# The attention's loop of four turns over three groups of heads, written out as twelve groups of straight code

## The chip, the cores and the metric

The kernel runs on one core of a Trainium2 chip. The metric is the device time of one execution in microseconds. Before the change three runs gave a median of 1996.15 us (1995.97 to 1996.78). The execution that the profiler recorded took 1994.75 us, of which 1992.6 us are the span from the first to the last instruction.

## The reference

Two blocks work on `x` of shape (4, 1024, 512) in float32. The first is a conditioned feed-forward block. The second is attention with 16 heads of width 32 over 1024 positions, with no mask:

```python
qkv = (h @ Wqkv.T + bqkv).reshape(B, N, num_heads, hd, 3)
energy = jnp.einsum('bhqd,bhkd->bhqk', q, k)
att = jax.nn.softmax(energy, axis=-1) / D ** 0.5
out = jnp.einsum('bhqk,bhkd->bhqd', att, v)
out = out @ Wp.T + bp
h1 = out + hidden
h2 = _sln(h1, w, ln_g, ln_b, Wg, bg, Wb, bb)
return h2 + h1
```

## The kernel before

The kernel has five stages one behind the other: setup, the feed-forward block (L0), the projection to q, k and v, attention, and the output projection with its normalization. Each stage gives every engine a program of its own; engines meet only at semaphores. No scheduler orders anything: the order on an engine is the order of the code.

Attention treats 64 (batch, head) pairs in 16 groups of four heads. One group is 16 steps, eight blocks of 128 keys for each of two halves of 512 queries. In a step PE (TensorE) does, in `group` of `attention_stage`:

- four energy products (`energies`, L1220), each into one PSUM bank, which ACT (ScalarE) turns into `probs` with an exponential (L1349);
- four products for the row maxima (`max_unit`, L1204), reduced by DVE (VectorE) at L1371, which run 13 steps ahead of the energies that use them, so that the last 13 steps of a group work on the maxima of the next one;
- the product with v of the step before (`av`, L1232), and half of a sum of the denominators (`den`, L1248), whose input POOL (GpSimd) adds up pairwise at L1468.

SP (SyncE) issues the transfers: the next q, k and v, and the detour of the maxima and denominators through other layouts. Three sets of buffers (`RING = 3`) are used in turn, so group g works in slot (g + 2) mod 3.

All five engines walk through the 16 groups with one helper, `groups(eng, group)` at L1080 to L1092. Group 0 stands alone. Groups 1 to 12 are a hardware loop of four turns (`eng.Fori(0, 4)`, L1087), whose body holds three groups, one for each slot. Groups 13 to 15 stand alone behind it. In the loop the group number is a register, so each wait for a value that depends on it needs register instructions ahead of it, at the line of the wait (L1203, L1219 and so on for PE). At the end of a turn an engine adds one to its counter and jumps back with a compare-and-branch, both recorded at L1087. The engines turn back each for itself, when its own code reaches the end; nothing joins them there.

Of the kernel before, what the change touches and what calls it, by code (L numbers as in the profile page):

```python
# [1000 lines left out]
def attention_stage(nc, sh, wp_t):  # L1001
# [11 lines left out]
    with ExitStack() as ctx:  # L1013
# [68 lines left out]
        def groups(eng, group):  # L1082

            group(0, 2, nth=0, first=True)
            with eng.Fori(0, 4) as k:  # L1087
                for i in range(RING):
                    group(3 * k + i + 1, i, nth=k + (i + 2) // RING)
            group(13, 0, nth=4)  # L1090
            group(14, 1, nth=5, load=False)
            group(15, 2, load=False, with_next=False)  # L1092
# [14 lines left out]
        def _(sp):  # L1107
# [76 lines left out]
            place_neg(0, RING - 1, 0)  # L1184
            load_group(2, 1)
            groups(sp, group)
            for half in range(QH):
                store(G - 1, half)
# [7 lines left out]
        def _(pe):  # L1196
# [111 lines left out]
            pe.wait_ge(ones_col_ready, 1)  # L1308
            pe.wait_ge(stack_loaded[RING - 1], LOADS)
            groups(pe, group)  # L1310
            av(G - 1, RING - 1, STEPS - 1)
            den(G - 1, PAIRS - 2, range(PARTS))
# [12 lines left out]
        def _(act):  # L1325
# [35 lines left out]
            act.wait_ge(wp_loaded, 16)  # L1361
            nc.scalar.copy(sh.wp[:, HI], wp_raw[:]).then_inc(wp_split, 1)
            groups(act, group)
            take_av(G - 1, 1)
            take_den(G - 1, 1)
# [384 lines left out]
```

## Time and profile before

| | before |
|---|---|
| median of 3 runs | 1996.15 us |
| the profiled execution | 1994.75 us |
| its span | 1992.6 us |
| PE busy | 1902.4 us, 95% |
| DVE busy | 1209.5 us, 61% |
| POOL busy | 1147.9 us, 58% |
| ACT busy | 809.2 us, 41% |
| DMA, mean over the span | 107 GB/s |
| granted TensorE clock, mean | 0.972 |

Busy time is the union of an engine's instructions. PE is busy for nearly the whole span, so what counts is how much of its time it stands still, and how much of it runs at the lower of its two clock levels. The granted clock is a share of 2.4 GHz: 1.00 is 2.4 GHz, 0.50 is 1.2 GHz, and a value between them is a stretch with a part at each. PE here means the matrix products and PEld the loading of their stationary operand, which runs beside them. An engine name with a q, as SPq or PEldq, stands for its sequencer, whose register, branch and semaphore instructions are not counted as busy.

### The profile page before, as it was taken

The numbers are of one execution on the slowest core, as the hardware profiler recorded it, in microseconds if no ns is written. First come the engines' busy times: TensorE is split into PE (matmuls) and PEld (weight loads), VectorE is DVE, ScalarE is ACT, GpSimd is POOL, SyncE is SP. The second block draws the span as 40 slices with busy tenths as digits, with TensorE's granted clock in tenths as the row PEclk, the third lists the DMA queues.
The fourth block names the chain that finished last, engine by engine and source line by source line (L and its number), as shares of the span: only waits on it lengthen the run. The fifth ranks groups of instructions, "written<-read, shape, count | busy, mean of one in ns | idle before, by whom it ended". The sixth has DMA issues, their size and how long they took to land. (4 is left out here: it accounts for less than half of the span.)

```text
span 1992.6 us, 31072 instructions
## 1 busy us (share of the span) xinstructions
PE 1902.4 (95%) x10520; PEld 1243.4 (62%) x10520; DVE 1209.5 (61%) x1510; ACT 809.2 (41%) x1373; POOL 1147.9 (58%) x589
## 2 busy tenths in 40 slices
PE   6599999999998999998999999999999999999995
PEld 1478888888886888885445544554554545554584
DVE  3556555655646554446666666666666666664289
ACT  1322123112312222221566656666666666666300
POOL 0574465466445121212477777777777777877545
PEclk9799999999999999997899999999999999999997
DMA  6301110101123555566344422344443334405293
GB/s 240 123 1 53 45 41 21 53 32 39 35 74 101 190 188 181 189 198 175 73 97 108 103 67 77 96 102 98 107 103 78 78 83 102 107 24 181 92 392 123
DMA packets 117704, 212.67 MB, mean 107 GB/s; under 512 B 18599, under 2 KB 36135, under 8 KB 117577
## 3 DMA queue, kind: packets, MB, share of 16 engines
q1 hardware_dynamic: 98828, 200.04, 33.7%
q10 hardware_dynamic: 18560, 10.94, 1.9%
q8 instruction: 78, 1.28, 0.3%
q14 instruction: 46, 0.37, 0.1%
q0 software_dynamic: 192, 0.05, 0.0%
HBM read 134.40 MB, written 75.80 MB: 105 GB/s over the span
## 5 line engine op out<-in xcount | busy, mean ns | idle before, releaser
L1371 DVE TENSOR_REDUCE at_mrow<-banks 128x1 f32<-128x1024 f32 x512 | 604.4, 1217 | 281.2 <-PE banks L1204 281.2
L1349 ACT ACTIVATE at_probs<-banks 128x512 f32<-128x512 f32 x1024 | 557.6, 597 | 333.7 <-PE banks L1220 314.4
L1468 POOL TENSOR_TENSOR at_pair<-at_probs 128x2048 f32<-128x2048 f32 x127 | 582.0, 4583 | 176.8 <-ACT at_probs L1349 176.7
L1220 PE MATMUL banks<-early_qs,early_ks 98*128 98x512 f32 x1024 | 443.8, 436 | 5.5 <-ACT at_probs L1349 5.5
L1204 PE MATMUL banks<-early_ks,early_qs 96*128 96x512 f32 x1024 | 377.5, 413 | 13.3 <-DVE at_mrow L1371 9.7
L1220 PEld LDWEIGHTS banks<-early_qs,early_ks 98*128 98x128 f32 x1024 | 192.4, 189 | 211.6 <-ACT at_probs L1349 106.8
L1232 PE MATMUL banks<-at_probs,at_v 128*32 128x512 f32 x2048 | 274.9, 609 | 0.9 <-ACT at_probs L1349 0.9
L1204 PEld LDWEIGHTS banks<-early_ks,early_qs 96*128 96x128 f32 x1024 | 199.1, 197 | 53.4 <-DVE at_mrow L1371 26.7
L67 PE MATMUL banks<-l_ht,l_weights 128*128 128x512 f32 x768 | 178.8, 392 | 5.5 <-ACT l_gt L574 5.5
L67 PE MATMUL banks<-qk_nt,l_weights 128*128 128x512 f32 x768 | 177.1, 392 | 3.0 <-ACT qk_gt L889 3.0
L67 PE MATMUL banks<-l_weights,l_hf 128*128 128x512 f32 x768 | 177.3, 390 | 0.0
L574 ACT ACTIVATE l_gt<-banks,mod 128x512 f32<-128x512 f32 x64 | 48.1, 778 | 314.3 <-PE banks L468 278.7
L67 PEld LDWEIGHTS banks<-l_ht,l_weights 128*128 128x128 f32 x768 | 144.6, 189 | 35.6 <-issue 5.8
L67 PEld LDWEIGHTS banks<-qk_nt,l_weights 128*128 128x128 f32 x768 | 145.3, 189 | 33.5 <-ACT qk_gt L889 3.2
L67 PEld LDWEIGHTS banks<-l_weights,l_hf 128*128 128x128 f32 x768 | 143.7, 188 | 29.5
L1248 PEld LDWEIGHTS banks<-at_pair,at_ones_col 128*32 128x32 f32 x2032 | 66.3, 110 | 138.9 <-issue 133.0
L1248 PE MATMUL banks<-at_pair,at_ones_col 128*32 128x256 f32 x2032 | 151.1, 381 | 0.0
L988 POOL TENSOR_TENSOR qk_nt<-qk_gt,qk_nt 128x512 fp32r<-128x512 f32 x32 | 43.0, 1363 | 156.2 <-DVE qk_nt L940 156.2
L898 ACT ACTIVATE qk_out<-banks,cols 128x512 fp32r<-128x512 f32 x64 | 44.1, 690 | 192.5 <-PE banks L67 186.4
L700 POOL TENSOR_TENSOR l_ht<-l_gt,l_ht 128x512 fp32r<-128x512 f32 x64 | 84.3, 1318 | 62.7 <-DVE l_ht L616 62.7
L583 ACT ACTIVATE l_gt<-banks,cols 128x512 f32<-128x512 f32 x96 | 64.7, 689 | 105.0 <-POOL l_hf L700 51.0
L700 POOL TENSOR_TENSOR l_hf<-l_gt,l_hf 128x512 fp32r<-128x512 f32 x64 | 82.7, 1293 | 40.6 <-DVE l_hf L616 40.6
(120 smaller groups left out, 1955.3 us busy)
## 6 DMA issues: line engine op xcount, KB each, us to landing
qk_scratch<-qk_out SPq DMA_DIRECT2D x64, 512.0 KB, 2.8
early_ks<-qk_scratch SPq DMA_DIRECT2D x48, 512.0 KB, 6.7
early_qs<-qk_scratch SPq DMA_DIRECT2D x96, 256.0 KB, 11.6
attn_scratch<-at_out SPq DMA_DIRECT2D x32, 512.0 KB, 2.7
o_a<-attn_scratch SPq DMA_DIRECT2D x32, 512.0 KB, 11.0
v_scratch<-qk_v ACTq DMA_DIRECT2D x32, 256.0 KB, 2.4
at_v<-v_scratch SPq DMA_DIRECT2D x16, 512.0 KB, 14.6
o_x<-x_scratch SPq DMA_DIRECT2D x8, 1024.0 KB, 14.3
```

The lines of the kernel that those rows point to most:

```text
L67: last = pe.matmul(out, stationary(a), moving(b), start=start and n == 0, stop=stop and n == len(TERMS) - 1)
L574: nc.scalar.activation(gt[:, k % 2, :], half[k][:], ACT.Identity, bias=sh.mod[:, 2 * which + 1, k, bass.ds(b, 1)], scale=sh.mod[:, 2 * whi ...
L583: nc.scalar.activation(gt[:, n % 2, :], halves[n][:], func, bias=sh.cols[:, col + m:col + m + 1]).then_inc(gt_full, 1)
L700: nc.gpsimd.tensor_tensor(dst[:, LO, i, :], gt[:, i % 2, :], dst[:, HI, i, :].bitcast(F32), ALU.subtract).then_inc(gt_lo, 1)
L898: nc.scalar.activation(qk[:, m, HI, :], ps[m][:], ACT.Identity, bias=sh.cols[:, C_BQ + m:C_BQ + m + 1]).then_inc(qk_hi, 1)
L1204: pe.matmul(e_ps[u % 2][:, keys, :], qs[0:96, slot, half, j, c * P:(c + 1) * P], ks[0:96, slot, j, keys * CH:(keys + 1) * CH], start=True, ...
L1220: pe.matmul(et[j % 2][:], ks[0:98, slot, j, (i % KC) * P:(i % KC + 1) * P], qs[0:98, slot, i // KC, j, :], start=True, stop=True).then_inc ...
L1232: last = pe.matmul(av_ps[rows, :], v[:, slot, kc, rows], probs[:, kc % 4, j, :], start=kc == 0, stop=kc == KC - 1)
L1248: last = pe.matmul(den_ps[HD * j:HD * (j + 1), cols], ones_col[:], psum2[:, pair % 2, j, cols], start=n == 0 and part == 0, stop=n == KC / ...
L1349: nc.scalar.activation(probs[:, i % 4, j, :], et[j % 2][:], ACT.Exp).then_inc(exp_done, 1)
L1371: nc.vector.tensor_reduce(mrow[:, half, u:u + 1], e_ps[u % 2], AX.XY, ALU.max).then_inc(max_done, 1)
L1468: nc.gpsimd.tensor_tensor(psum2[:, pair % 2], probs[:, a], probs[:, a + 1], ALU.add).then_inc(pair_ready, 1)
```

## The change

One line of the helper changes, for all five engines alike. The four turns are no longer a loop of the hardware: Python's `range` runs when the program is built, and the twelve groups are emitted one behind the other, with group numbers that are constants.

```diff
@@ -1084,7 +1084,7 @@
             group(0, 2, nth=0, first=True)
-            with eng.Fori(0, 4) as k:
+            for k in range(4):
                 for i in range(RING):
                     group(3 * k + i + 1, i, nth=k + (i + 2) // RING)
             group(13, 0, nth=4)
```

The program of PE before, at the back edge of the loop (the last step of a turn, the counter, the branch, and the first products of group 13, which the last turn falls through to):

```order
L1219 REGISTER_ALU
L1220 MATMUL banks<-early_qs,early_ks 128x512
L1203 REGISTER_ALU
L1204 MATMUL banks<-early_ks,early_qs 128x512
L1219 REGISTER_ALU
L1220 MATMUL banks<-early_qs,early_ks 128x512
L1204 MATMUL banks<-early_ks,early_qs 128x512
L1087 REGISTER_ALU
L1087 COMPARE_AND_BRANCH
L1204 MATMUL banks<-early_ks,early_qs 128x512
L1220 MATMUL banks<-early_qs,early_ks 128x512
```

The program of PE now, at the place where the last step of a group meets the first of the next:

```order
L1220 MATMUL banks<-early_qs,early_ks 128x512
L1204 MATMUL banks<-early_ks,early_qs 128x512
L1220 MATMUL banks<-early_qs,early_ks 128x512
L1204 MATMUL banks<-early_ks,early_qs 128x512 x2
L1220 MATMUL banks<-early_qs,early_ks 128x512
L1204 MATMUL banks<-early_ks,early_qs 128x512
L1220 MATMUL banks<-early_qs,early_ks 128x512
```

The products and their order are the same; counter, branch and the register instructions are gone. On ACT the head of the loop before reads as follows (`at_probs` is the exponential of an energy bank, `at_av_sb` the copy of the product with v):

```order
L1349 ACTIVATE at_probs<-banks 128x512 x16
L1087 UNCONDITIONAL_BRANCH
L1087 ISA
L1346 ISA
L1348 ISA
L1349 ACTIVATE at_probs<-banks 128x512
L1348 REGISTER_ALU
L1349 ACTIVATE at_probs<-banks 128x512
L1328 ISA
L1331 REGISTER_ALU
L1332 ACTIVATE at_av_sb<-banks 128x512
L1348 REGISTER_ALU
```

ACT's program now at the same place:

```order
L1349 ACTIVATE at_probs<-banks 128x512 x18
L1332 ACTIVATE at_av_sb<-banks 128x512
L1349 ACTIVATE at_probs<-banks 128x512 x14
L1339 COPY at_den_sb<-banks 128x512
L1349 ACTIVATE at_probs<-banks 128x512 x18
```

Here too no activation moves; the register instructions between them are gone. The straight form of a group is not new to the program: groups 0 and 13 to 15 had it before.

## Rows read from the trace of the kernel before

**Rows 1.** The page: span, and busy time of each engine.
```profile
span 1992.6 us, 31072 instructions
PE 1902.4 (95%) x10520; PEld 1243.4 (62%) x10520; DVE 1209.5 (61%) x1510; ACT 809.2 (41%) x1373; POOL 1147.9 (58%) x589
```

**Rows 2.** Waits from 1009 to 1867 us: who waited for whom, total, times, longest.
```profile
ACT at_probs L1349 <- PE banks L1220: 273.6, 274, 2.6
DVE at_mrow L1371 <- PE banks L1204: 260.9, 231, 3.2
...
PE banks L1204 <- DVE at_mrow L1371: 6.6, 3, 2.3
PE banks L1220 <- ACT at_probs L1349: 5.5, 12, 0.6
```

**Rows 3.** Stretches, groups 1 to 14, each from its first energy product (columns named).
```profile
core 0: us, PE busy (x) PEld busy (x) DVE busy (x) ACT busy (x) POOL busy (x), PEclk, DMA share, GB/s
1009.45:1065.99 56.54, 56.54 (x387) 28.35 (x387) 38.86 (x39) 36.71 (x69) 43.66 (x14) 1.00 0.39 95
...
1122.53:1181.58 59.05, 56.79 (x387) 28.40 (x387) 40.14 (x39) 37.07 (x69) 46.55 (x16) 1.00 0.39 91
1181.58:1239.68 58.10, 58.10 (x388) 28.76 (x386) 37.77 (x38) 36.36 (x68) 41.27 (x13) 0.97 0.38 93
...
1296.22:1355.10 58.88, 56.78 (x388) 28.40 (x388) 40.04 (x39) 37.07 (x69) 46.46 (x16) 1.00 0.37 92
1355.10:1413.14 58.04, 58.04 (x388) 29.12 (x386) 37.76 (x38) 36.48 (x68) 41.29 (x13) 0.97 0.39 93
...
1469.68:1528.69 59.01, 56.79 (x388) 28.39 (x387) 40.04 (x39) 37.07 (x69) 46.39 (x16) 1.00 0.37 91
1528.69:1585.19 56.50, 56.50 (x387) 28.34 (x386) 37.76 (x38) 36.37 (x68) 41.34 (x13) 1.00 0.39 96
...
1698.27:1754.80 56.53, 56.53 (x388) 28.35 (x387) 38.84 (x39) 36.72 (x69) 43.79 (x14) 1.00 0.39 95
1754.80:1811.32 56.52, 56.52 (x387) 28.34 (x387) 38.83 (x39) 36.71 (x69) 44.09 (x14) 1.00 0.09 30
sum 801.87, PE 795.29 PEld 398.21 DVE 544.35 ACT 514.14 POOL 616.94; mean PE 56.81 PEld 28.44 DVE 38.88 ACT 36.72 POOL 44.07
```

**Rows 4.** Timeline of PE at the first branch: start, us, instruction, idle before, releaser.
```profile
1178.37 0.40 PE L1220 MATMUL banks<-early_qs,early_ks 98*128 98x512 f32 x1
1178.61 0.39 PE L1204 MATMUL banks<-early_ks,early_qs 96*128 96x512 f32 x1
1181.26 0.49 PE L1204 MATMUL banks<-early_ks,early_qs 96*128 96x512 f32 x1 [2.26 <-DVE at_mrow L1371]
```

**Rows 5.** Line L1087: durations in ns (least, median, most), first and last start.
```profile
L1087 PEldq COMPARE_BRANCH  x4: 83/3636/3732, 1177.2 to 1696.4; - x4
L1087 ACTq COMPARE_BRANCH  x4: 40/53/53, 1178.9 to 1698.1; - x4
L1087 DVEq COMPARE_BRANCH  x4: 50/56/63, 1179.1 to 1698.3; - x4
L1087 POOLq COMPARE_BRANCH  x4: 40/45/45, 1179.6 to 1698.8; - x4
```

**Rows 6.** Timeline of DVE at the first branch.
```profile
1179.03 1.23 DVE L1371 TENSOR_REDUCE at_mrow<-banks 128x1 f32<-128x1024 f32 x1 [1.17 <-PE banks L1204]
```

**Rows 7.** Stretches of one step: undisturbed, and the first behind each of three branches.
```profile
1239.68:1243.20 3.52, 3.52 (x25) 1.76 (x25) 2.34 (x3) 2.76 (x6) 2.87 (x2) 1.00 0.13 22
1181.58:1186.68 5.10, 5.10 (x25) 2.18 (x24) 1.26 (x2) 2.42 (x5) 4.20 (x2) 0.67 0.17 43
1355.10:1360.19 5.09, 5.09 (x26) 2.57 (x25) 1.26 (x2) 2.66 (x5) 4.22 (x2) 0.66 0.33 64
1528.69:1532.20 3.51, 3.51 (x26) 1.76 (x24) 1.27 (x2) 2.43 (x5) 3.51 (x2) 1.00 0.13 40
```

**Rows 8.** DMA queues that carry instructions: packets, MB, share of 16 engines.
```profile
q8 instruction: 78, 1.28, 0.3%
q14 instruction: 46, 0.37, 0.1%
```

## The prediction

> **What bounds the kernel now.** I read the page's busy times first. PE is busy for 1902.4 of 1992.6 us, no other engine for more than 1209.5 us [rows 1]. In the attention the waits confirm who leads: ACT stood 273.6 us and DVE 260.9 us waiting for PE, while PE stood 6.6 us behind DVE, in three pieces, and 5.5 us behind ACT, in twelve [rows 2]. So PE sets the pace, and only what makes PE idle or slows it can move the time.
>
> Then I laid one stretch over each group, from the first energy product of one group to that of the next [rows 3]. All hold the same work (387 or 388 products), so their lengths may be compared. Two are straight code already: group 13 takes 56.53 us and group 14 takes 56.52 us. In the loop group 1 takes 56.54 us, and of the twelve looped groups seven lie between 56.50 and 56.54. Five are longer: group 3 (59.05), 4 (58.10), 6 (58.88), 7 (58.04) and 9 (59.01). The loop turns back at the ends of groups 3, 6 and 9; at the end of group 12 it falls through. The long groups are exactly those that end or begin at a taken branch.
>
> The timeline of PE shows what happens there [rows 4]. The product that starts at 1178.61 is the last of its turn's code; the next starts at 1181.26, with 2.26 us of idle time ahead of it. The rows of the branch give the reason [rows 5]: on PE's sequencer the compare-and-branch has a median of 3636 ns and a most of 3732 ns over four, and the least is 83 ns. One of the four is not taken, three are. The first began at 1177.2 and so lasted until 1180.9; the sequencer had run ahead of the array, and the array worked off what was queued, until 1179.0, before it stood.
>
> **Whether the branch is the cause.** The trace names a DVE reduction (L1371) as the releaser of the 2.26 us. This must be decided, because if PE truly waited for DVE, the wait would stay when the branch goes. The code speaks against it: `max_unit` n waits for reduction n - 2 only, as two pairs of banks are in use. The reduction that stands next to the stall ran from 1179.03 to 1180.26 [rows 6] and belongs to the product that ended at 1179.0, thus, if the next unit is n, to unit n - 1. The one that was needed lay before it. Even the later one was over 1.0 us before PE restarted. The branch, over at 1180.9, fits the restart at 1181.26.
>
> **The change part by part.**
>
> 1. *Three taken branches on PE.* The groups that end at one are longer than group 13 by 59.05 - 56.53 = 2.52, 58.88 - 56.53 = 2.35 and 59.01 - 56.53 = 2.48 us. Sum 7.35 us. Of this, the idle time is 6.6 us, the three pieces [rows 2]; the rest is the slower restart of the first products (0.49 us instead of 0.39 for the first [rows 4]). All of it is on the path, since PE is what the others wait for.
>
> 2. *The clock behind the branches.* Right behind the stall of the first and second branch the granted clock falls: the first step of group 4 takes 5.10 us at a mean of 0.67, that of group 7 takes 5.09 us at 0.66, while an undisturbed step takes 3.52 us at 1.00 [rows 7]. A mean of 0.67 is a stretch of which two thirds run at the 1.2 GHz level. Behind the third branch the step takes 3.51 us at 1.00, so that stall cost no clock. By groups: 58.10 - 56.53 = 1.57 and 58.04 - 56.53 = 1.51 us. Sum 3.08 us. With no idle stretch on PE ahead of it the reason for the fall is gone; groups 13 and 14, which no stall precedes, run at 1.00 [rows 3].
>
> 3. *Register instructions.* They go from between the products of twelve groups on PE, and likewise on the other engines. Looped groups of 56.54 us stand against 56.53 in straight code, so they cost 0.01 us a group at most: they run on the sequencers, beside the products already queued, and the array hides them. Over seven undisturbed groups this is under 0.1 us. If that cover were gone (a PE program held up at its sequencer), groups 13 and 14 would have been visibly shorter; they are not.
>
> 4. *Branches on the other engines.* Their compare-and-branch takes 40 to 63 ns by the rows [rows 5]; ACT and DVE wait for PE far more than that each step. ACT's stop after its branch may be longer than the instruction shows, but it lies within PE's own and goes with it. I cost it at nothing.
>
> 5. *Fetching of longer programs.* Straight code has to bring in each group's instructions, but the loop does it as well: the instruction queues moved 78 and 46 packets, 1.28 and 0.37 MB in all [rows 8], for a share of 0.3 and 0.1% of the engines. The unknown is whether a fetch can come late in straight code. Bounds: nothing, as groups 13 and 14 show, up to one stall of 2.26 us in every one of twelve groups, 27.1 us. I take nothing, because two straight groups of the same code are the nearest rows, and they ran beside the same loads (DMA share 0.39 in group 13 as in the loop).
>
> The sum in one piece: the fourteen stretches of groups 1 to 14 sum to 801.87 us; fourteen times 56.53 is 791.42; the difference is 10.45 us [rows 3]. By parts it is 7.35 + 3.08 = 10.43. I take 10.4 us.
>
> At this place two rules of the Trainium skill point in opposite directions. "Advanced Engine Details and Errata", section on control flow timing, gives a compare-and-branch about 108 ns. By that alone four of them are worth 0.4 us, and the change would do nothing that can be seen; the trace agrees only for the branch that is not taken. "Runtime: NRT & Kernel Launch", section on the mechanics of instruction fetch, says that fetching ahead is purely sequential and that a taken branch to a target outside the window fetched forces a fetch before execution can go on. With that the trace agrees on PE, at its 3636 ns median, and not for the short instruction records of the other engines; it also speaks for part 5, as straight code stays sequential.
>
> **Against which time.** The profiled execution took 1994.75 us, 1992.6 in its span and 2.15 around it, which the change does not touch. Less 10.4 this is 1984.35, with a span of 1982.2. The median of the timed runs is 1996.15, 1.40 us above. This may be a cost that stays (then 1996.15 - 10.4 = 1985.75) or a fall of the clock behind the third branch, which the profiled execution escaped and which costs 1.5 us (then it goes too, and the median comes to 1984.3). Between them I say 1985.0.
>
> **Rivals.**
>
> *The clock's losses stay.* The falls might not be caused by the stall but come in the attention anyway, by a count of the chip's own. For: one of three stalls had none. Against: groups 1, 10, 13 and 14 stand at 1.00 [rows 3], and both falls begin at the step behind a stall. Then only part 1 is won: 1996.15 - 7.35 = 1988.8.
>
> *The wait is there anyway.* PE's idle time is DVE's, as the releaser is named, or another engine is late in the same place. Then the 6.6 us stay and the clock with them; only register instructions go: 1996.0, no change. Against it stand the order of units above, and that no group without a branch, of the same code, has this idle time.
>
> *Straight code starves PE of instructions.* The program is now sequential for 900 us; the fetches of PE, of four other engines and the loads of SP use the same DMA engines. If PE's next block comes late once in a group, at the beginning of the loads, it costs 2.26 us twelve times, 27.1, and the net is 27.1 - 10.4 = 16.7 us slower: 2012.9. It decides from the fifth late block on (5 x 2.26 = 11.3 against 10.4). For: nothing in the trace is as long as the new straight stretch. Against: groups 13 to 14.
>
> *The change does nothing*, because the loop is built again: excluded, as the order of PE has neither counter nor branch there.
>
> **How the numbers follow.** The forecast, 10 to 12 us won, gets 0.88; the clock's losses staying 0.06; the wait staying 0.03; starving 0.02; and 0.01 for a gain beyond. The range must hold the two anchors (1984.3 and 1985.75), the spread of the runs before (0.8 us from 1995.97 to 1996.78) on either side, one more or less fall of the clock (1.5 us) elsewhere in the kernel, as everything behind the loop moves against it, and it reaches to the first rival: 1982.5 to 1988.8. A measurement of this kernel tells a change of 0.2% (4 us) from none. Both the forecast and the first rival are beyond it: faster 0.95, no change 0.03, slower 0.02.
>
> **What the profile after would show.** No row at L1087; the branch's 3.6 us gone and the idle time at L1204 behind DVE with it. All groups from 1 to 14 at 56.5 us from first energy product to first energy product; the long five at the same value as their neighbours. PEclk at 1.00 in every one of them. PE's busy time down by about 3.9 us (3.1 of slow steps, and 0.26 at each restart: 56.79 busy in group 3 against 56.53), the rest of the gain in its idle time. Instruction packets no more than before, since fewer register instructions are run. What would prove me wrong: stretches that still are 58 or 59 us long, at any group (part 1 or 2 wrong); a lowered clock with no stall ahead of it (part 2); a group pace away from 56.53 (part 3); or idle time on PE that nothing releases, at changing places (part 5).

## The result, and the profile after

| | before | after |
|---|---|---|
| median, 4 runs each on the same chip | 1996.06 us | 1983.86 us |
| lowest to highest | 1994.56 to 1996.78 | 1983.63 to 1984.56 |
| the profiled execution | 1994.75 us | 1984.56 us |
| its span | 1992.6 us | 1982.8 us |

The ratio after to before is 0.9941, with a 95% interval of 0.9928 to 0.9953: 12.2 us less by the medians, 9.4 to 14.4 us by the interval. The two profiled executions differ by 10.2 us, and their spans by 9.8.

The page of the profile after, its first lines and the instruction queues:

```profile
span 1982.8 us, 28225 instructions
PE 1898.3 (96%) x10520; PEld 1242.2 (63%) x10520; DVE 1208.9 (61%) x1510; ACT 809.0 (41%) x1373; POOL 1147.7 (58%) x589
...
q8 instruction: 68, 1.11, 0.2%
q14 instruction: 40, 0.33, 0.0%
```

Every engine still runs exactly the work of [rows 1]; 2847 instructions of the sequencers are gone. PE's busy time fell by 4.1 us (3.9 was forecast), the rest of the gain is idle time that is gone. Fewer instruction packets are fetched than before [rows 8], although the program is longer.

The groups of the attention after the change, each from its first energy product to that of the next (groups 1, 3, 4, 6, 7, 9, 10, 13 and 14; columns as in [rows 3]):

```profile
1009.61:1066.15 56.54, 56.54 (x388) 28.36 (x387) 38.84 (x39) 36.71 (x69) 44.09 (x15) 1.00 0.39 95
1122.68:1179.22 56.54, 56.54 (x387) 28.36 (x387) 38.84 (x39) 36.71 (x69) 44.15 (x15) 1.00 0.39 95
1179.22:1235.76 56.54, 56.54 (x387) 28.36 (x387) 38.84 (x39) 36.72 (x69) 44.10 (x15) 1.00 0.40 95
1292.29:1348.83 56.54, 56.54 (x387) 28.35 (x387) 38.84 (x39) 36.71 (x69) 44.08 (x15) 1.00 0.39 95
1348.83:1405.36 56.53, 56.53 (x387) 28.35 (x387) 38.84 (x39) 36.72 (x69) 43.73 (x15) 1.00 0.39 95
1461.89:1518.43 56.54, 56.54 (x388) 28.35 (x387) 38.84 (x39) 36.71 (x69) 44.08 (x15) 1.00 0.39 95
1518.43:1574.95 56.52, 56.52 (x387) 28.35 (x387) 38.83 (x39) 36.70 (x69) 44.07 (x14) 1.00 0.39 95
1688.03:1744.57 56.54, 56.54 (x388) 28.36 (x387) 38.85 (x39) 36.72 (x69) 44.32 (x15) 1.00 0.40 95
1744.57:1801.11 56.54, 56.54 (x388) 28.35 (x387) 38.85 (x39) 36.71 (x69) 43.73 (x15) 1.00 0.10 30
```

The five long stretches of [rows 3] (59.05, 58.10, 58.88, 58.04, 59.01) have become 56.53 or 56.54. All fourteen groups now lie between 56.52 and 56.54, and the clock stands at 1.00 in all of them. From the start of group 1 to that of group 13 the engines took 1698.27 - 1009.45 = 688.82 us before and take 1688.03 - 1009.61 = 678.42 us now: 10.40 us less.

PE's timeline at the place of the first branch (columns as in [rows 4]) now has no gap. The double row at 1178.75 holds the last product of group 3's code and the first of group 4's:

```profile
1178.52 0.40 PE L1220 MATMUL banks<-early_qs,early_ks 98*128 98x512 f32 x1
1178.75 0.63 PE L1204 MATMUL banks<-early_ks,early_qs 96*128 96x512 f32 x2
1179.22 0.41 PE L1220 MATMUL banks<-early_qs,early_ks 98*128 98x512 f32 x1
```

### The profile page after: what moved, and what is told of

It is laid out like the page before. It is cut to its first block and busy times, and to the rows that moved or that the text cites. A ratio compares the mean times of both kernels' runs of the same rounds, so it can differ in the third digit from the quotient of the medians.

```text
span 1982.8 us, 28225 instructions
## 1 busy us (share of the span) xinstructions
PE 1898.3 (96%) x10520; PEld 1242.2 (63%) x10520; DVE 1208.9 (61%) x1510; ACT 809.0 (41%) x1373; POOL 1147.7 (58%) x589
## 5 line engine op out<-in xcount | busy, mean ns | idle before, releaser
L1204 PE MATMUL banks<-early_ks,early_qs 96*128 96x512 f32 x1024 | 375.9, 412 | 6.7 <-PEq L754 3.5
L1204 PEld LDWEIGHTS banks<-early_ks,early_qs 96*128 96x128 f32 x1024 | 198.2, 196 | 45.3 <-DVE at_mrow L1371 18.8
L616 DVE CAST l_ht<-l_gt 128x512 fp32r<-128x512 f32 x64 | 50.6, 790 | 92.1 <-ACT l_gt L583 49.8
```

Of the source, the lines that this page charges most:

```text
L616: nc.vector.tensor_copy(dst[:, HI, i, :], gt[:, i % 2, :]).then_inc(gt_hi, 1)
L1204: pe.matmul(e_ps[u % 2][:, keys, :], qs[0:96, slot, half, j, c * P:(c + 1) * P], ks[0:96, slot, j, keys * CH:(keys + 1) * CH], start=True, ...
```

## The experiments

Each kernel is compared with runs of the kernel before on the same chip. Its median there was 1995.49 us for the questions on each engine's loop and the two turns, 1997.09 for the stop without a branch and the last pair of smaller bodies, and 1996.60 for the others. The sweep of sizes is a single run, of which only the branches are read. What decides is the ratio and the trace. Where I say "straight", the twelve groups of the attention are written out. The first two edits are shown against the kernel before, the others against the kernel after. Numbers from a trace that stand in no row here (starts of groups, packets, instructions in a turn) are counted in the trace of the run named.

**Which engine's loop costs.** The helper got a flag, so that each engine can have its own form:

```diff
-        def groups(eng, group):
+        def groups(eng, group, looped=False):
...
-            with eng.Fori(0, 4) as k:
+            def turn(k):
                 for i in range(RING):
                     group(3 * k + i + 1, i, nth=k + (i + 2) // RING)
+            if looped:
+                with eng.Fori(0, 4) as k:
+                    turn(k)
+            else:
+                for k in range(4):
+                    turn(k)
```

*PE alone straight.* The other four call it with `True`.

> PE alone has straight code; ACT, DVE, POOL and SP keep the loop of four turns. Theory A (each engine has its own stop at a taken branch, and the second longest, ACT's, was hidden behind PE's): in the trace before, ACT's sequencer went on 2.5 to 2.8 us after its branch, against 3.6 to 3.8 on PE and 0.3 on the others. ACT will now be late by over 2 us three times, PE waits for its exponentials (idle time at L1220 behind ACT), and the three groups that end at a branch take about 58.5 us instead of 56.5. Time 1988 to 1993. Theory B (PE's branch was the whole cost; ACT idles over 1 us a step and absorbs its stop): time as with all engines straight, 1983.9, all groups 56.5 us.

Measured: 1989.51 us (1987.69 to 1990.32), ratio 0.9967 (0.9955 to 0.9979). About half of the change's gain. One row of the waits from 1009 to 1860 us, then the timeline around the first branch (L1227, L1356 are the energy product and the exponential, moved by seven lines), then the stretches of groups 3 and 4:

```profile
PE banks L1227 <- ACT at_probs L1356: 8.4, 15, 1.0
```

```profile
1182.25 0.61 PE L1255 MATMUL banks<-at_pair,at_ones_col 128*32 128x256 f32 x8
...
1183.18 1.08 ACT L1356 ACTIVATE at_probs<-banks 128x512 f32<-128x512 f32 x2 [2.30 <-PE banks L1239]
...
1183.83 0.51 PE L1227 MATMUL banks<-early_qs,early_ks 98*128 98x512 f32 x1 [0.97 <-ACT at_probs L1356]
```

```profile
1123.98:1180.53 56.55, 56.55 (x387) 28.34 (x387) 38.95 (x39) 36.76 (x69) 44.16 (x15) 1.00 0.40 95
1180.53:1238.40 57.87, 56.89 (x387) 28.26 (x387) 38.87 (x39) 36.53 (x69) 44.01 (x15) 1.00 0.39 93
```

ACT stands for 2.30 us. The trace puts that down to PE, but PE's energies were ready; ACT's sequencer went on 2.57 to 2.62 us after its branch. PE then waits 0.97 us for ACT, and the group is 1.32 us longer than its neighbour. Three such groups (4, 7 and 10, which begin behind a branch, not those that end at one, as I had written) are 4.0 us in this trace. My figure of 58.5 us for them was too high. This execution is 5.5 us longer than the profiled one of the kernel after; most of the other 1.5 us lies ahead of group 1, which starts 1.3 us later, and that start differs as much among kernels whose code is alike up to there. So the time came inside the range of Theory A partly by what isn't ACT's stop. Theory B falls.

*PE alone looped.* Only PE calls it with `True`.

> PE alone keeps the loop; the other four engines have straight code. Theory A (PE's stop of 3.6 us sets the time while all loop, the others' lie within it): time as before the change, 1996 (1995 to 1997), three stretches of PE idle time of 2.1 to 2.3 us ahead of L1204. Theory B (the register instructions and branches of the other engines carry a part): 1990 or less.

Measured: 1995.30 us (1993.79 to 1996.60), ratio 0.9996 (0.9987 to 1.0005): no change against before. The row of PE's branches, three taken and one not:

```profile
L1092 PEldq COMPARE_BRANCH  x4: 83/3490/3851, 1177.7 to 1698.3; - x4
```

So the loops of the other four engines cost nothing as long as PE loops. Theory A holds, with three stops of 2.07 to 2.45 us. The trace puts two of them down to DVE and the longest to nothing. The clock fell behind the first, where group 4 took 59.18 us, and behind the third (group 10: 58.06), and not behind the second (group 7: 56.51).

*ACT alone looped.*

> ACT alone keeps the loop. Theory A (ACT's stop is what comes second, and DVE, POOL and SP with 0.3 us cost nothing): the same time as with only PE straight, within 1 us, so 1988 to 1993. Theory B (the loops of the other three cost something too): clearly less than with only PE straight. If ACT's stop is absorbed, both stand at 1983.9.

Measured: 1989.03 us (1988.73 to 1989.80), ratio 0.9968 (0.9955 to 0.9980), within 0.5 us of the kernel in which all but PE loop. Groups 4, 7 and 10 are the long ones again, with 4.0 us together over straight code. Of those four engines only ACT's loop matters.

**Fewer taken branches.** All engines loop, in two turns of six groups:

```diff
-            with eng.Fori(0, 4) as k:
-                for i in range(RING):
-                    group(3 * k + i + 1, i, nth=k + (i + 2) // RING)
+            with eng.Fori(0, 2) as k:
+                for i in range(2 * RING):
+                    group(6 * k + i + 1, i % RING, nth=2 * k + (i + 2) // RING)
```

> All engines loop, but in two turns of six groups, so one branch is taken instead of three. Theory A (the cost goes by taken branches): a third of 12.2 us, from 2.4 (no fall of the clock) to 4.0 (with one): 1986.3 to 1987.9, one stretch of idle time on PE at the end of group 6, all other groups 56.5 us. Theory B (the cost goes by looped groups, by register instructions or by length of the loop): near 1996, since twelve groups are still looped.

Measured: 1988.54 us (1987.89 to 1989.04), ratio 0.9965 (0.9951 to 0.9978). The stretches of groups 5 to 8:

```profile
1235.83:1292.37 56.54, 56.54 (x388) 28.35 (x387) 38.86 (x39) 36.72 (x69) 44.56 (x15) 1.00 0.39 95
1292.37:1351.88 59.51, 56.90 (x388) 28.46 (x388) 40.05 (x39) 37.06 (x69) 44.43 (x15) 1.00 0.39 92
1351.87:1409.84 57.97, 57.97 (x387) 28.75 (x386) 37.87 (x38) 36.48 (x68) 43.28 (x14) 0.97 0.39 93
1409.84:1466.38 56.54, 56.54 (x387) 28.35 (x387) 38.87 (x39) 36.72 (x69) 44.44 (x15) 1.00 0.40 95
```

One taken branch, one pair of long groups, 2.97 + 1.43 = 4.4 us, and all other groups at the pace of straight code though they are looped. The cost goes by taken branches, as Theory A has it. The time is 0.6 us above my range; this one branch lasted longer (4032 ns) than any of the three taken ones of before (3576, 3697 and 3732; the median of 3636 in [rows 5] counts the one that is not taken). The longer turn also did something to the other engines: DVE with 465 instructions in it and SP with 397 now stood 3.0 and 2.7 us behind their branch, where 234 and 202 had brought 0.3. Both pauses lie beside PE's.

**Near targets.** Straight code, with a little loop on PE ahead of each of the twelve groups:

```diff
                 for i in range(RING):
+                    if near:
+                        with eng.Fori(0, 2):
+                            eng.sem_inc(sh.pe_passed, 1)
                     group(3 * k + i + 1, i, nth=k + (i + 2) // RING)
```

> All engines straight, and on PE ahead of each of the twelve groups a loop of two turns around one semaphore increment: twelve taken branches whose targets lie a few instructions back. Theory A (what costs is a target that PE's sequencer has to fetch again): each takes 0.2 to 0.3 us on the sequencer, as those of the shorter loops in the trace before, hidden behind queued products: 1983.9, within 1 us. Theory B (a taken branch costs about 3.6 us on PE wherever it goes): twelve times about 2.4 us idle, 2013 or more.

Measured: 1984.84 us (1983.40 to 1985.87), ratio 0.9943 (0.9930 to 0.9957), the same as all straight. The row of the 24 branches, twelve of them taken:

```profile
L1090 PEldq COMPARE_BRANCH  x24: 76/144/227, 1006.3 to 1628.8; - x24
```

A taken branch as such costs nothing here. Theory B falls.

**The same stop without a branch.** Straight code, and on PE alone:

```diff
                     group(3 * k + i + 1, i, nth=k + (i + 2) // RING)
+                if stop and k < 3:
+                    for _ in range(24):
+                        eng.sem_inc(sh.pe_passed, 1)
```

> All engines straight; on PE alone, at the ends of groups 3, 6 and 9, where the taken branches were, stand 24 semaphore increments, which hold PE's sequencer 0.153 us each by the run before, 3.7 us in all, as long as the branch did. No branch, no fetching again. Theory A (the branch costs by the idle time that it makes, and the granted clock falls by the idle time, not by the branch): three stretches of 2.1 to 2.4 us idle, a lowered clock behind two or three of them, time as before the change, 1994 to 1997. Theory B (the clock's falls come from the branch or the fetch): idle time only, 1983.9 + 7.3 = 1991, clock 1.00 throughout.

Measured: 1995.49 us (1993.36 to 1996.66), ratio 0.9993 (0.9984 to 1.0002): no different from before. The stretches of groups 3, 4, 6, 7, 9 and 10:

```profile
1121.89:1180.63 58.74, 56.77 (x387) 28.38 (x387) 40.03 (x39) 37.07 (x69) 46.36 (x16) 1.00 0.37 91
1180.63:1238.71 58.08, 58.08 (x388) 29.03 (x386) 37.74 (x38) 36.47 (x68) 41.21 (x13) 0.97 0.38 93
1295.23:1354.09 58.86, 56.78 (x388) 28.38 (x388) 40.03 (x39) 37.07 (x69) 45.94 (x16) 1.00 0.38 91
1354.09:1410.56 56.47, 56.47 (x387) 28.33 (x386) 37.75 (x38) 36.36 (x68) 42.45 (x14) 1.00 0.40 95
1467.10:1525.87 58.77, 56.77 (x388) 28.38 (x388) 40.03 (x39) 37.06 (x69) 46.44 (x16) 1.00 0.37 91
1525.87:1583.91 58.04, 58.04 (x388) 28.67 (x386) 37.75 (x38) 36.39 (x68) 41.77 (x14) 0.97 0.38 93
```

The pattern of [rows 3] is back without a branch, and no packet of the queue that carries PE's instructions (q8, see below) starts in any of the three stops: 58.7 to 58.9 us where PE stands, and 58.0 to 58.1 behind it where the clock falls. This time the second stop is the one without a fall; in the trace before it was the third. So PE's idle time is enough to bring the fall, and a stop of this length does not always do so. Theory B falls.

**How large a body may be.** Two pairs of kernels shorten PE's part of a turn. They leave work out, so each is compared with its own counterpart. In the first pair most products of the denominators and half of those with v are left out, and the rest overwrite instead of adding up (so do the last products behind group 15, not shown):

```diff
-                for j in range(HG):
+                for j in range(HG if kc == 0 else 2):
...
-                                     start=kc == 0, stop=kc == KC - 1)
+                                     start=True, stop=True)
...
-                    for j in range(HG):
+                    for j in range(HG if n == 0 else part):
...
-                                         start=n == 0 and part == 0, stop=n == KC // 2 - 1 and part == PARTS - 1)
+                                         start=True, stop=True)
```

*With PE looped:*

> PE alone loops, four turns, three groups, with fewer PE instructions in each: most products of the denominators (L1248) and half of those with v are left out, and the rest of these overwrite instead of adding up. A turn has about 1760 PE instructions instead of 2614; the loops of the first stages, with 1369 and 672, had a stop of 0.3 us. Theory A (the stop comes when the turn doesn't fit what PE's sequencer keeps): compare-and-branch 0.2 us instead of 3.6, no idle time of 2 us, and the time of its straight counterpart within 1 us. Theory B (a branch back over so many instructions costs in any case, or costs by distance): 2.4 us or more for the branch, and 5 us or more above the counterpart.

*All straight:*

> The counterpart: all engines straight, with the same PE instructions left out in the attention. It is there for the comparison alone. By Theory A its time is that of the looped one within 1 us; by Theory B it is 5 us or more less.

Measured: looped 1969.28 us (1961.86 to 1971.13), straight 1949.15 (1947.20 to 1950.79), 20.1 us apart. Theory A, as I had put its bound, was wrong: with 1774 instructions a turn PE's taken branches are as long as ever.

```profile
L1092 PEldq COMPARE_BRANCH  x4: 83/3510/3816, 1167.8 to 1671.7; - x4
```

The 20.1 us are more than the change itself was worth, and only part of them is explained. The two traces are 11.1 us apart, and the six groups around the three branches differ by more, 341.3 against 325.8 us: 5.2 us a branch, where the kernel before lost 3.5. Behind the stop at each branch (1.9 to 2.4 us) PE here stands a second time, for 0.9 to 1.7 us ahead of the product with v, and the clock falls behind all three branches. The traced looped execution is also the fastest of its four, by 7.4 us. The others were granted a lower mean clock (0.966 to 0.969 against 0.970), so more falls are likely, but no trace shows them.

The long branches left two explanations open, a smaller bound than I had thought or a cost of the attention's own. So I measured the branch by itself, behind the last product of the straight kernel, with bodies of nothing but semaphore increments (ACT has the same with its own sizes):

```diff
+            for size in (600, 1200, 1400, 1500, 1600, 1700, 2000):
+                with pe.Fori(0, 2):
+                    for n in range(size):
+                        pe.sem_inc(fill[n % 5], 1)
```

> All loops as after the change; behind its last product PE runs loops of two turns whose bodies are 600, 1200, 1400, 1500, 1600, 1700 and 2000 semaphore increments, and ACT, idle by then, runs loops with 120, 230, 260, 290, 320, 350, 400, 470 and 560. Each loop takes one branch back. Only the length of the branch (PE) or of the pause behind it (ACT) is read; the time of the whole is much longer and means nothing. The run with the smaller body had shown that PE's 3.6 us stay at 1774 instructions, where 1369 had 0.3 us. Theory A (the stop depends on the number of instructions in the body, whatever they are): PE about 0.2 us up to 1200 or 1400 and 3 us or more from 1600 or 1700 on; ACT 0.3 us up to 230 and 2.5 us or more at 400 at the latest. Theory B (it hangs on the attention's stage, its DMA traffic or its place in the program, not on size): all alike, short or long. Theory C (it grows with the distance): a steady rise over the sizes.

The taken branches on PE with 1200, 1600, 1700 and 2000 increments, one row each:

```profile
L1565 PEldq COMPARE_BRANCH  x1: 208/208/208, 2324.8 to 2324.8; - x1
...
L1565 PEldq COMPARE_BRANCH  x1: 208/208/208, 3645.1 to 3645.1; - x1
...
L1565 PEldq COMPARE_BRANCH  x1: 4558/4558/4558, 4151.5 to 4151.5; - x1
...
L1565 PEldq COMPARE_BRANCH  x1: 3765/3765/3765, 4725.3 to 4725.3; - x1
```

The others (600, 1400, 1500) took 227, 207 and 218 ns. On ACT the instruction itself is always short and the pause stands behind it. Its rows with 290 and with 320 increments:

```profile
L1572 ACTq COMPARE_BRANCH  x1: 45/45/45, 1981.6 to 1981.6; - x1
L1572 ACTq EVENT_SEMAPHORE  x1: 17/17/17, 1984.5 to 1984.5; - x1
...
L1572 ACTq COMPARE_BRANCH  x1: 45/45/45, 2028.7 to 2028.7; - x1
L1572 ACTq EVENT_SEMAPHORE  x1: 17/17/17, 2029.0 to 2029.0; - x1
```

| increments in ACT's body | 120 | 230 | 260 | 290 | 320 | 350 | 400 | 470 | 560 |
|---|---|---|---|---|---|---|---|---|---|
| us from branch to next instruction | 0.26 | 0.25 | 0.24 | 2.91 | 0.26 | 2.39 | 2.39 | 2.52 | 2.39 |

Short or long, with nothing between: Theory A, with PE's bound between 1600 and 1700 instructions and ACT's between 260 and 350, where it isn't sharp (290 is long, 320 short). Each size was run once. There is neither a steady rise nor anything of the attention in it. Why 290 was long stays open; where a body lies in the program was not varied.

*Below the bound, in place.* With only a quarter of the products with v kept in groups 1 to 12 (`for j in range(HG if isinstance(g, int) and not 0 < g < 13 else 1)`) and the denominators cut as above, a turn has 1534 instructions. PE looped:

> PE alone loops, four turns, three groups; in the looped groups most products of the denominators and three quarters of those with v are left out, so that a turn has about 1534 PE instructions. The sweep kept the short branch up to 1603 and had the long one from 1703 on. Theory A (size decides here too): the three taken branches last 0.2 us, no idle time of 2 us on PE, and the time is that of its straight counterpart within 1 us. Theory B (in the attention a branch is long whatever the body): 3 to 4 us each, and 10 us or more above the counterpart.

All straight:

> The counterpart for the comparison: all engines straight, with the same PE instructions left out in groups 1 to 12. Theory A: as the looped one within 1 us. Theory B: 10 us or more less than the looped one.

Measured: looped 1949.30 us (1944.57 to 1949.50), straight 1947.38 (1946.92 to 1949.76); against before 0.9752 (0.9739 to 0.9766) and 0.9758 (0.9745 to 0.9772), intervals that overlap. The medians are 1.9 us apart, more than the 1 us I gave, but their ranges overlap, and in the two traces groups 1 to 14 take 757.8 us looped and 758.0 us straight. The branches decide:

```profile
L1092 PEldq COMPARE_BRANCH  x4: 76/208/211, 1168.9 to 1655.6; - x4
```

The same loop in the same place has branches of 0.21 us once its body is small enough.

The packets of the instruction queues show what the long branch waits for. Queue q8 carries PE's instructions: in the sweep it brings a packet of 16 KB every 39.4 us, the time of some 257 of PE's increments. In the kernel before such a packet starts 1.0 to 1.1 us after each taken branch began (1178.27, 1352.02, 1525.41) and takes 0.9 to 1.2 us; with 1774 instructions a turn one starts 1.0 to 1.5 us after each. With 1534 none starts from 1165.5 to 1677.0 us, over all three taken branches, and none from 253.0 to 558.2 in the kernel before, over those of the feed-forward block (1369 instructions). So a body below the bound is kept, and a larger one is fetched again.

**All loops of the kernel straight.** Each `with eng.Fori(a, b) as k:` became `for k in range(a, b):`, in the feed-forward block and the projection too.

> All loops of the kernel as straight code, those of the feed-forward block and of the projection to q, k, v too. Theory A (a branch costs only where its target was no longer kept): the branches of these loops take 0.2 us on PE and no product waits for them, so nothing is won: 1983.9, within 1 us. Theory B (each taken branch is worth 3 to 4 us): four more are gone, 1970 or less.

Measured: 1984.65 us (1983.03 to 1987.56), ratio 0.9943 (0.9929 to 0.9957): nothing beyond the change. In the kernel after, these loops' PE bodies are below the bound, and the branch row of the feed-forward block shows it:

```profile
L557 PEldq COMPARE_BRANCH  x3: 76/220/238, 261.4 to 536.7; - x3
```

No version that does the whole work beats the changed kernel.

## Why the prediction was right

*The branch as the cause of PE's idle time, against the named releaser:* shown. The idle pieces at L1204 are gone with PE's branch, come back with PE's loop alone, and come back with 24 increments in place of the branch, while DVE has the same work in all of them. The length of 3636 ns that I read for the branch is the median of four with the one that is not taken; the three taken ones lasted 3576, 3697 and 3732 ns. Nothing in the sum hangs on it.

*Step 1, three taken branches, 7.35 us, and step 2, the clock behind two of them, 3.08 us:* shown in size, 10.40 us measured over groups 1 to 12 and 10.37 over 1 to 14, against 10.45 worked out. The rest of the spans' difference lies elsewhere and nearly cancels: group 0 took 56.12 us instead of 57.42 (a shorter part of it at the lower clock level), began 1.46 us later, and what follows the start of group 13 took 0.4 us more. Nothing gives these to the change: over the traces of kernels that do the whole work group 0 takes 55.92 to 57.60 us, looped and straight alike.

*Step 3, register instructions at no cost:* shown by the two turns of six groups, looped at 56.54 us a group.

*Step 4, the other engines' branches at nothing:* right for this change, where all go together. I wrote that ACT's stop might be longer than its instruction shows and lies within PE's; alone it is worth some 5 us (1989.0 and 1989.5 against 1983.9), of which the traces show 4.0 in the groups. It was the next thing late, and had only PE's loop been written out, about half of the gain would have been lost to it.

*Step 5, no late fetch in straight code:* right; no group after is off its pace and fewer packets were fetched. My ground for it was thinner than I wrote: of the two straight groups only group 13 ran beside the loads, as group 14 has a DMA share of 0.09. In the kernel after groups 1 to 13 ran at 56.52 to 56.54 us beside the loads.

*The time.* For a profiled execution I had 1984.35 and 1984.56 came. For the median I stood between two anchors, 1984.3 and 1985.75, and said 1985.0; 1983.86 came. The gain of the medians, 12.2 us, is 1.8 above the 10.4 of the traces, well within the interval. One more fall of the clock in the timed runs of before than in its trace would fit, since a stop brings a fall in some cases and not in others, but this is not shown: no trace covers those runs, and the mean clocks on record give it no support (of 42 executions of the kernel before beside the experiments, 23 with a mean of 0.972 have a median of 1996.3 us and 14 with 0.974 one of 1996.4). That 1985.0 came as close as 1.1 us owes something to luck, as it is the middle between two guesses at this remainder.

*The rival in which the clock's losses stay:* it fell with the straight groups, all at 1.00, and with the stops without a branch. The rival in which the wait is there anyway fell likewise, and starved straight code did not come.

At the place where I weighed two rules of the Trainium skill, the runs refine both. The 108 ns that the Trainium skill gives in "Advanced Engine Details and Errata" for a compare-and-branch lie between one that is not taken on PE (76 to 83 ns) and one that is taken within the bound (0.21 us), and far from one beyond it. The Trainium skill's "Runtime: NRT & Kernel Launch", section on the mechanics of instruction fetch, gives the engines' instruction memory as 2048 instructions for PE and 512 for most others. By that figure alone the body of 1774 would have fitted; measured, the bound is between 1600 and 1700 on PE and between 260 and 350 on ACT. Why it lies below the figure no run here shows. The rule on taken branches that I took from the same section holds beyond the bound, on PE by the packets behind each long branch. It speaks of a window of two pages, which the section gives as 256 instructions each; with that the traces do not agree, as PE kept bodies of 1369 and 1534 instructions.

## What to carry to other kernels

Look in the trace for stretches of equal work that are not equally long, and at whether the odd ones sit at the turn of a loop; here the price of a hardware loop was one stop for each taken branch, only if the body was too large to be kept (over some 1600 instructions on TensorE, some 300 on ScalarE), and only on the path. A body below that bound may stay a loop: writing those of the first stages out won nothing. When a loop is written out, do it on every engine at once, as the next engine's stop (here ScalarE's) takes over when the longest is gone.

## What the runs showed of the hardware

- A taken compare-and-branch beyond the bound shows on PE in the instruction's own duration (3.3 to 4.6 us against 0.21), on ACT only as a pause of 2.3 to 3.0 us behind an instruction of 45 to 53 ns, and on DVE and SP, in the turn of six groups, as one of 3.0 and 2.7 us. A row that lists durations alone hides it.
- On PE a 16 KB packet of its instruction queue starts 1.0 to 1.1 us after each such branch of the kernel before, and none starts over the branches of a turn with 1534 instructions.
- The trace gives an idle time behind such a branch to whatever semaphore stands in the next instruction's wait (DVE in [rows 4], PE for ACT's 2.30 us), though that had been reached before.
- A stop that left TensorE idle for 2.0 to 2.5 us lowered the granted clock from 2.4 to 1.2 GHz in two of three cases in each of three traces (before, PE alone looped, the stop without a branch), for 1.5 to 1.6 us of loss five times and 2.65 us once. The length of the stop does not sort them: 1.97 us brought a fall, 2.22 us none. ACT's stops, which left TensorE idle for 0.8 to 1.2 us, did so in none of six.
